# Value products of 64 rows with p copied by ScalarE alone, and the shifted feed-forward input sent behind the scores

## The chip, the cores and the metric

One NeuronCore of a Trainium2 chip. The time is device microseconds, the median of three runs. The kernel is one launch with no work on the host.

## The reference

The input x is 2 sequences of 1024 tokens of 128 features (2048 tokens, or 16 tiles of 128 tokens). A stack of six transformer layers runs twice on it, with one scan layer between the two passes:

- x = x + 0.5 * stack(layernorm(x))
- x = x + scan_layer(layernorm(x)): a 128x128 projection, a first-order recurrence over the tokens, and another 128x128 projection
- x = x + 0.5 * stack(layernorm(x))

Each stack layer does, in float32:

- shift: the upper 64 features of a token are replaced by those of the token before it
- local attention with 16 heads of 64: q, k, v = shifted x @ Wqkv (128 x 3072). q and k are scaled to unit length and rotated. Windows of 32 tokens attend to themselves and to the window before (32 queries against 64 keys), with a causal mask, softmax, and the product with v; then @ Wo (1024 x 128) and the residual
- feed-forward: shift again, layernorm, @ W1 (128 x 682), a * gelu(gate), @ W2 (341 x 128), residual.

## The kernel before

A step handles one tile of 128 tokens at each stage of a software pipeline. There are 12 passes of a layer over 16 tiles, so T = 192 tiles and about 198 steps, fully unrolled. In step s an engine works on several tiles at once: tile s-1 is projected to q and k (L_QKV), s-2 gets its values and scores (L_S), s-3 its softmax (L_SM), s-4 the product p v and the output projection (L_AV, L_WO), s-5 the first half of the feed-forward (L_F), s-6 the second (L_F2), and tile s is transposed in (L_X). "k.on(L)" starts the part of a stage, and "k.wait(sem, L)" waits until the semaphore's event has happened for the tile at that stage. Each engine executes its part of the step in the written order of its function step(k); between engines only these semaphores order anything. No planner is involved. Around step 102, over some twenty steps, the scan layer is threaded in (middle(k)): more work for VectorE and GpSimd.

One step on each engine, in order:

- TensorE: q/k projection chunks 1 and 0 (line 484), transposes of q (495), the products p v (attend, 539), chunks 2 and 3 (484), transposes of k (495), output projection (594), transposes of p (602), transpose of the normalised feed-forward input xn (607), second feed-forward product (622), values chunks 1 and 0 (490), transpose of the next tile (639), first feed-forward products (503), mask (519) and scores (527).
- ScalarE: squares (673), exp (686), copies of qT, oT, kT out of PSUM (691, 695, 711), xn (715), its half of the copy of p (722), xnT (727), the values (677), gelu with its table load (740), and the shifted next tile xsT (747 to 750).
- VectorE: swp and rot for chunks 0 and 1 (861, 867) with bn_aggr (932) and the epsilon (937) between them, the row sums of p (940), nb (945), the reciprocal (949), two reductions of the squares (954, 957) with chunk 3 between them, chunk 2, a chain of small reciprocal-root operations (816 to 848) with the two residual additions (969, 979) among them, its half of the copy of p (992), middle(k), the gate product hT (1001), the row maximum (1008) and the subtraction (1011), and bn_stats of the shifted input xs2 (1016).
- GpSimd: a power for the layernorm (1074), the normalisation of p (1078), rot+swp (1084), and rot times the inverse norm (1093).
- SyncE's DMA queue: vb (the values of the window before, 447 and 448), weights (357, 361), and the shift, four transfers from Z to xs2 (405 to 408), issued once the first residual addition (969, semaphore v_z1) is done.

The operand pT of the products p v has 128 rows, of which half are zeros: the four windows of a tile are handled in pairs, a pair shares one product with K = 128, and the block that belongs to the other window is zero. pT is cleared once and only the non-zero quarters are written, rows 0 to 63 by ScalarE (722) and rows 64 to 127, with neighbouring 32-blocks exchanged, by VectorE (992). A product has 64 columns of weights (the values) and 64 moving columns, 32 products a step. A float32 product shows as two LDWEIGHTS and two MATMUL records in the trace, a transpose as one of each.

Semaphores that the steps of the prediction name: v_ab[c] says that rot chunk c is written; values(k, 0) needs v_ab[2] and values(k, 1) needs v_ab[3], since they write over the same PSUM bank. a_v is the copied values, a_xT the transposed next tile, p_S the scores, p_O the products p v, v_nb the bias for xn, d_xs2 the arrival of the shift.

Of the kernel before, what the change touches and what calls it, by code (L numbers as in the profile page):

```python
# [57 lines left out]
def macaron(nc, x_in, w_in, w_out, b_out, w_qkv, q_scale, k_scale, w_o,  # L58
            w_1, w_2, b_2, c_cols, c_rope, c_mask, c_ident, out):
    with ExitStack() as ctx:  # L60
# [16 lines left out]
        pT = sb("pT", [PAIRS * 2, 2, 2, WIN])  # L77
# [64 lines left out]
        c_pz = sem("c_pz")  # L142
        v_pT = sem("v_pT")
# [210 lines left out]
        def _(sp):  # L354
# [81 lines left out]
            def step(k):  # L436
                if k.reg is not None:

                    for lag in (L_X, L_WO):
                        k.slot(lag), k.slot(lag, 0, P // 2), k.slot(lag, 1, P // 2)  # L440
                if k.on(L_SM):


                    k.wait(a_v[0], L_SM)
                    k.wait(p_O, L_AV)
                    par = k.parity(L_SM)
                    sp.dma_start(vb[WIN:P, :], va[0:P - WIN, par, :]).then_inc(d_vb, 16)
                    sp.dma_start(vb[0:WIN, :], va[P - WIN:P, 1 - par, :]).then_inc(d_vb, 16)
                load_weights(k)
                if k.on(L_WO):  # L450


                    k.wait(v_z1, L_WO)
                    shift(k, L_WO, xs2[:, :], d_xs2)
                if k.reg is None and k.s >= OUT:
                    t = k.s - OUT
                    sp.wait_ge(f_out, t + 1)
                    sp.dma_start(out[t // POS, (t % POS) * P:(t % POS + 1) * P, :], xb[:, t, :]).then_inc(d_out, 16)
# [9 lines left out]
        def _(pe):  # L468
# [62 lines left out]
            def attend(k):  # L531
                par = k.parity(L_AV)
                for p in range(PAIRS):
                    o4 = ops[:, p // 4, (p % 4) * P:(p % 4 + 1) * P].rearrange("p (t g i) -> p t g i", t=2, g=2)
                    for g in range(2):
                        for hp in range(2):
                            at = (2 * p + hp) * DH
                            v = vb[:, at:at + DH] if g == 0 else va[:, par, at:at + DH]
                            last = mm(o4[hp * DH:(hp + 1) * DH, :, g, :], v,  # L539
                                      pT[:, 2 * p + g, hp, :, :].rearrange("p t i -> p (t i)"),  # L540
                                      start=True, stop=True, skip_group_check=True)
                last.then_inc(p_O, 1)

            def step(k):
# [87 lines left out]
                if k.on(L_X):  # L632
                    k.wait(v_z1, L_WO)
                    if k.mid(M_T) is not None:
                        k.wait_mid(m_xn, M_T)
                        tr(ops[:, 0, 2 * P:3 * P], mx_n[:, :], idf[:, :])
# [31 lines left out]
        def _(act):  # L668
# [10 lines left out]
            def step(k):  # L679
# [12 lines left out]
                if k.on(L_AV):  # L692
                    k.wait(p_O, L_AV)
                    k.wait(p_wo, L_WO + 1)
                    cp(oT[:, :, :], ops[:, :, :].rearrange("p b (a x) -> p (b a) x", x=P)).then_inc(a_oT, 1)  # L695
# [20 lines left out]
                if k.on(L_SM):  # L716

                    k.wait(p_pT, L_SM)
                    k.wait(p_O, L_AV)
                    if k.s == L_SM:  # L720
                        act.wait_ge(c_pz, 1)
                    cp(pT[0:DH, :, :, 0, :], tps[0:DH, :, :].rearrange("p c (g h i) -> p (c g) h i", g=2, i=WIN)).then_inc(a_pT, 1)  # L722
# [20 lines left out]
                if k.on(L_X):  # L743
# [3 lines left out]
                    cp(xsT[0:hf, par, 0:P], ops[0:hf, 0, P:2 * P])  # L747
                    cp(xsT[hf:P, par, 1:P + 1], ops[hf:P, 0, P:2 * P])
# [3 lines left out]
                if k.mid(M_T) is not None:  # L752

                    k.wait(p_xT, L_X)
                    cp(mx_t[:, :], ops[:, 0, 2 * P:3 * P]).then_inc(m_xT, 1)
# [27 lines left out]
        def _(dve):  # L783
# [135 lines left out]
            def step(k):  # L919
# [22 lines left out]
                if k.on(L_F):  # L942
                    k.wait(g_rstd, L_F)
                    k.wait(a_xn, L_F + 1)
                    v.tensor_scalar(nb[:, 0:1], mv[:, 0:1], rt2[:, 1:2], -1.0, ALU.mult, ALU.mult).then_inc(v_nb, 1)
                if k.on(L_SM):
                    k.wait(v_sum, L_SM)
                    k.wait(g_nrm, L_SM + 1)
                    v.reciprocal(rr[:, :], rs[:, :]).then_inc(v_rec, 1)  # L949
                if k.on(L_QKV):  # L950
# [7 lines left out]
                    rotate(k, 3, False)  # L958
                    rsqrt(k, 1)
# [23 lines left out]
                if k.on(L_SM):  # L983

                    if k.s == L_SM:
                        dve.wait_ge(c_pz, 1)
                    k.wait(p_pT, L_SM)
                    k.wait(p_O, L_AV)
                    src = tps[DH:P, :, :]
                    swapped = bass.AP(src.tensor, src.offset + WIN,  # L990
                                      [list(src.ap[0]), [2 * WIN, 2 * PAIRS], [-WIN, 2], [1, WIN]])
                    v.tensor_copy(pT[DH:P, :, :, 1, :], swapped).then_inc(v_pT, 1)
# [60 lines left out]
        def _(pool):  # L1053
# [16 lines left out]
            def step(k):  # L1070
                if k.on(L_F):
                    k.wait(v_ve, L_F)
                    k.wait(a_xn, L_F + 1)
                    g_.tensor_tensor(rt2[:, 1:2], rt2[:, 0:1], half[:, 0:1], ALU.pow).then_inc(g_rstd, 1)  # L1074
                if k.on(L_SM):
# [3 lines left out]
                                     ALU.mult).then_inc(g_nrm, 1)  # L1079
                if k.on(L_QKV):  # L1080
# [73 lines left out]
            def between(s):  # L1154

                if s == 0:
                    g_.memset(pT[:, :, :, :, :], 0.0).then_inc(c_pz, 1)
# [72 lines left out]
```

## Time and profile before

| | us |
|---|---|
| median of 3 runs | 3302.99 (3298.94 to 3304.68) |
| the profiled execution | 3302.78 |
| its span, first to last instruction | 3301.0 |

TensorE was granted 0.994 of its full clock on average. The page gives PE 3177.7 us of busy time, DVE 2994.8, ACT 2543.2 and POOL 2229.6. PE is TensorE's matmuls, PEld its weight loads, DVE is VectorE, ACT ScalarE, POOL GpSimd, SP SyncE. A busy PE is a modelled figure, since matmuls overlap. In a timeline row the first number is the start and the second the length in us, then come engine, line, operation, output and input, and in brackets the idle time before it with what ended it. On VectorE and ScalarE a record lasts some 0.1 us beyond the start of the next one when they run back to back, so the distance of two starts, and not the length, is what an operation costs there.

### The profile page before, as it was taken

The numbers are of one execution on the slowest core, as the hardware profiler recorded it, in microseconds if no ns is written. First come the engines' busy times: TensorE is split into PE (matmuls) and PEld (weight loads), VectorE is DVE, ScalarE is ACT, GpSimd is POOL, SyncE is SP. The second block draws the span as 40 slices with busy tenths as digits, with TensorE's granted clock in tenths as the row PEclk, the third lists the DMA queues.
The fourth block names the chain that finished last, engine by engine and source line by source line (L and its number), as shares of the span: only waits on it lengthen the run. The fifth ranks groups of instructions, "written<-read, shape, count | busy, mean of one in ns | idle before, by whom it ended". The sixth has DMA issues, their size and how long they took to land. (4 is left out here: it accounts for less than half of the span.)

```text
span 3301.0 us, 125954 instructions
## 1 busy us (share of the span) xinstructions
PE 3177.7 (96%) x50984; PEld 2377.1 (72%) x51176; DVE 2994.8 (91%) x7143; ACT 2543.2 (77%) x4144; POOL 2229.6 (68%) x1454
## 2 busy tenths in 40 slices
PE   7999999999999999999889999999999999999998
PEld 3777777777777777776667777777777777777776
DVE  7999999999899999999999998899999999999995
ACT  3877878777787777777667777788777777887775
POOL 6666666666666666667777766666666666666663
PEclk9999999999999999999999999999999999999999
DMA  4111111111111111111111111111111111111111
GB/s 124 44 48 44 48 45 48 45 48 44 47 45 48 45 48 45 47 44 39 37 37 47 45 48 45 40 48 46 45 44 48 45 48 45 48 45 48 47 52 38
DMA packets 134996, 155.84 MB, mean 47 GB/s; under 512 B 75539, under 2 KB 108439, under 8 KB 134423
## 3 DMA queue, kind: packets, MB, share of 16 engines
q1 hardware_dynamic: 129815, 144.42, 15.9%
q8 instruction: 413, 6.77, 0.9%
q10 hardware_dynamic: 4608, 3.34, 0.4%
q14 instruction: 160, 1.31, 0.1%
HBM read 33.38 MB, written 1.05 MB: 10 GB/s over the span
## 5 line engine op out<-in xcount | busy, mean ns | idle before, releaser
L1084 POOL TENSOR_TENSOR rot<-rot,swp 128x1024 f32<-128x1024 f32 x384 | 907.2, 2363 | 132.5 <-DVE rot L867 132.5
L484 PE MATMUL proj<-wq,xsT 128*128 128x512 f32 x1536 | 773.4, 622 | 55.9 <-DVE hT L1001 22.4
L673 ACT ACTIVATE sq<-proj 128x512 f32<-128x512 f32 x768 | 437.6, 596 | 400.6 <-PE proj L484 387.3
L1093 POOL TENSOR_TENSOR rot<-rot,rn 128x1024 f32<-128x1024 f32 x384 | 724.6, 1910 | 0.0
L1074 POOL TENSOR_TENSOR rt<-rt,half 128x1 f32<-128x1 f32 x192 | 105.8, 551 | 743.1 <-DVE rt L937 743.1
L861 DVE TENSOR_TENSOR swp<-proj,tab 128x512 f32<-128x512 f32 x768 | 522.0, 680 | 9.4 <-ACT sq L673 5.1
L867 DVE TENSOR_TENSOR rot<-proj,tab 128x512 f32<-128x512 f32 x768 | 518.9, 676 | 1.7 <-PE tps L495 1.6
L495 PEld LDWEIGHTS tps<-idf,rot 128*128 128x128 f32 x3072 | 362.6, 141 | 207.1 <-issue 205.1
L1078 POOL TENSOR_TENSOR prob<-prob,rr 128x1024 f32<-128x1024 f32 x192 | 365.8, 1905 | 174.7 <-DVE rr L949 174.7
L484 PEld LDWEIGHTS proj<-wq,xsT 128*128 128x128 f32 x1536 | 257.5, 189 | 293.0 <-issue 138.1
L495 PE MATMUL tps<-idf,rot 128*128 128x128 f32 x3072 | 402.0, 274 | 3.5 <-POOL rot L1093 1.9
L594 PE MATMUL ops<-wo,oT 128*128 128x128 f32 x3072 | 376.3, 276 | 4.0 <-ACT oT L695 4.0
L539 PE MATMUL ops<-pT,vb 128*64 128x64 f32 x6144 | 379.3, 225 | 0.0
L490 PE MATMUL proj<-wq,xsT 128*128 128x512 f32 x768 | 369.5, 601 | 3.5 <-DVE rot L867 3.3
L539 PE MATMUL ops<-pT,va 128*64 128x64 f32 x6144 | 369.6, 222 | 0.0
L594 PEld LDWEIGHTS ops<-wo,oT 128*128 128x128 f32 x3072 | 359.8, 193 | 4.3 <-issue 4.2
L527 PEld LDWEIGHTS sps<-kT,qT 64*32 64x32 f32 x24576 | 258.4, 105 | 121.5 <-issue 121.1
L722 ACT COPY pT<-tps 64x1024 f32<-64x1024 f32 x192 | 193.2, 1006 | 187.3 <-PE tps L602 187.3
L1001 DVE SCALAR_TENSOR_TENSOR hT<-proj,cols,fg 114x128 f32<-114x128 f32 (+1 forms) x576 | 166.8, 345 | 187.4 <-issue 179.1
L539 PEld LDWEIGHTS ops<-pT,vb 128*64 128x64 f32 x6144 | 311.6, 138 | 32.9 <-issue 32.6
L527 PE MATMUL sps<-kT,qT 64*32 64x64 f32 x24576 | 296.2, 225 | 33.3 <-issue 33.2
L503 PEld LDWEIGHTS proj<-xnT,w 128*114 128x114 f32 (+1 forms) x2304 | 273.5, 178 | 73.7 <-issue 67.9
(104 smaller groups left out, 6164.6 us busy)
## 6 DMA issues: line engine op xcount, KB each, us to landing
vb<-va SPq DMA_DIRECT2D x192, 384.0 KB, 3.5
vb<-va SPq DMA_DIRECT2D x192, 128.0 KB, 3.6
wq<-in_L_ffn_Wqkv SPq DMA_DIRECT2D x95, 192.0 KB, 3.4
xs<-Z SPq DMA_DIRECT2D x192, 32.0 KB
wo<-in_L_ffn_Wo SPq DMA_DIRECT2D x94, 64.0 KB, 2.8
xs<-Z SPq DMA_DIRECT2D x192, 28.0 KB
xs<-Z SPq DMA_DIRECT2D x192, 3.8 KB
xs<-Z SPq DMA_DIRECT2D x192, 0.2 KB
```

Source lines behind the costliest of these rows:

```text
L484: mm(proj[:, c % 2, :], xsT[:, k.parity(L_QKV), 0:P], wq2[:, bass.ds(w + c * 512, 512)], start=True, stop=True).then_inc(p_qkv[c], 1)
L490: mm(proj[:, c, :], xsT[:, k.parity(L_S), 0:P], wq2[:, bass.ds(w + (4 + c) * 512, 512)], start=True, stop=True).then_inc(p_v[c], 1)
L495: last = tr(tps[:, p, :], rot[:, g * INNER + p * P:g * INNER + (p + 1) * P], idf[:, :])
L527: last = mm(sps[to:to + WIN, ty, p * 64:(p + 1) * 64], qT[rows, p, w * WIN:(w + 1) * WIN], kT[rows, p, at:at + 2 * WIN], start=False, stop ...
L539: last = mm(o4[hp * DH:(hp + 1) * DH, :, g, :], v, pT[:, 2 * p + g, hp, :, :].rearrange("p t i -> p (t i)"), start=True, stop=True, skip_g ...
L594: last = mm(ops[:, 0, 0:P], oT[:, p, :], wo[:, bass.ds(w + p * P, P)], start=(p == 0), stop=(p == PAIRS - 1))
L673: fn(sq[:, c * 512:(c + 1) * 512], proj[:, c % 2, :], ACT.Square).then_inc(a_sq[c], 1)
L861: v.tensor_tensor(halves(swp[:, c * 512:(c + 1) * 512]), swapped, tab[:, bass.ds(po + (2 * g + 1) * POS * DH, DH)] .rearrange("p (a d) -> ...
L867: v.tensor_tensor(heads(rot[:, c * 512:(c + 1) * 512]), heads(src), tab[:, bass.ds(po + 2 * g * POS * DH, DH)].unsqueeze(1) .to_broadcast( ...
L1078: g_.tensor_tensor(pr, pr, rr[:, :].unsqueeze(2).to_broadcast([P, HEADS, 2 * WIN]), ALU.mult).then_inc(g_nrm, 1)
L1084: g_.tensor_tensor(r, r, swp[:, g * INNER:(g + 1) * INNER], ALU.add).then_inc(g_add[g], 1)
L1093: g_.tensor_tensor(r, r, rn[:, g * HEADS:(g + 1) * HEADS].unsqueeze(2) .to_broadcast([P, HEADS, DH]), ALU.mult).then_inc(g_nm[g], 1)
```

## The change

1. pT becomes 128 x 8 x 128 without padding. Each product p v of K = 128 with 64 moving columns is split in two of K = 64 with 32 moving columns, one for each row half t, which write to two different PSUM banks. There are 64 products a step in place of 32.
2. The copy of p out of PSUM is one ScalarE copy of 128 x 1024; VectorE's copy (992), its semaphore v_pT, and the clearing of pT with c_pz are gone. oT is read with another order of its elements.
3. The shift's four transfers wait for p_S of the same step as well.
4. bn_stats (1016) moves from the end of VectorE's step to the next step behind the rotations of chunks 0 and 1. bn_aggr follows the row sums, the epsilon the reciprocal, and nb comes behind the last rotation of chunk 3. On GpSimd the power (1074) comes behind the normalisation of p (1078).
5. On TensorE the transpose of xn comes behind the second feed-forward product, and the transposes of the next tile go to the bank of tps in place of ops, behind waits for a_kT and a_pT in place of v_z1.

```diff
@@ sync, step
                     k.wait(v_z1, L_WO)
+                    k.wait(p_S, L_S)
                     shift(k, L_WO, xs2[:, :], d_xs2)
@@ tensor, attend
-                    o4 = ops[:, p // 4, (p % 4) * P:(p % 4 + 1) * P].rearrange("p (t g i) -> p t g i", t=2, g=2)
...
-                            v = vb[:, at:at + DH] if g == 0 else va[:, par, at:at + DH]
-                            last = mm(o4[hp * DH:(hp + 1) * DH, :, g, :], v,
-                                      pT[:, 2 * p + g, hp, :, :].rearrange("p t i -> p (t i)"),
-                                      start=True, stop=True, skip_group_check=True)
+                            for t in range(2):
+                                o4 = ops[:, t, p * 64:(p + 1) * 64].rearrange("p (g i) -> p g i", g=2)
+                                at = (2 * p + hp) * DH
+                                rows = slice(t * DH, (t + 1) * DH)
+                                v = vb[rows, at:at + DH] if g == 0 else va[rows, par, at:at + DH]
+                                to = (2 * g + (hp ^ t)) * WIN
+                                last = mm(o4[hp * DH:(hp + 1) * DH, g, :], v, pT[rows, p, to:to + WIN],
+                                          start=True, stop=True, skip_group_check=True)
@@ tensor, step
-                    k.wait(v_pT, L_AV)
...
-                if k.on(L_F):
-                    k.wait(a_xn, L_F)
-                    k.wait(v_sub, L_S + 1)
-                    tr(sps[:, 1, 0:P], xn[:, :], idf[:, :]).then_inc(p_xnT, 1)
                 if k.on(L_F2):
...
                     last.then_inc(p_f2, 1)
+                if k.on(L_F):
+                    k.wait(a_xn, L_F)
+                    k.wait(v_sub, L_S + 1)
+                    tr(sps[:, 1, 0:P], xn[:, :], idf[:, :]).then_inc(p_xnT, 1)
...
                 if k.on(L_X):
-                    k.wait(v_z1, L_WO)
+                    k.wait(a_kT, L_S)
+                    k.wait(a_pT, L_SM)
...
-                    tr(ops[:, 0, P:2 * P], Z[:, bass.ds(k.slot(L_X), P)], idf[:, :]).then_inc(p_xT, 1)
+                    tr(tps[:, 4, :], Z[:, bass.ds(k.slot(L_X), P)], idf[:, :]).then_inc(p_xT, 1)
@@ scalar, step
-                    cp(pT[0:DH, :, :, 0, :], tps[0:DH, :, :].rearrange("p c (g h i) -> p (c g) h i", g=2, i=WIN)).then_inc(a_pT, 1)
+                    cp(pT[:, :, :], tps[:, :, :]).then_inc(a_pT, 1)
@@ vector, step
                     rotate(k, 0, True)
                     rotate(k, 0, False)
-                if k.on(L_F):
-                    k.wait(v_bn, L_F)
-                if k.on(L_QKV):
                     rotate(k, 1, True)
-                if k.on(L_F):
-                    v.bn_aggr(mv[:, :], st[:, :]).then_inc(v_mv, 1)
-                if k.on(L_QKV):
                     rotate(k, 1, False)
                 if k.on(L_F):
-                    k.wait(v_mv, L_F)
-                    v.tensor_scalar(rt2[:, 0:1], mv[:, 1:2], 1e-5, None, ALU.add).then_inc(v_ve, 1)
+                    k.wait(d_xs2, L_F, per=64)
+                    v.bn_stats(st[:, :], xs2[:, :]).then_inc(v_bn, 1)
                 if k.on(L_SM):
                     k.wait(a_exp, L_SM)
                     v.tensor_reduce(rs[:, :], prob[:, :, :, :].rearrange("p a t j -> p (a t) j"), AX,
                                     ALU.add).then_inc(v_sum, 1)
                 if k.on(L_F):
-                    k.wait(g_rstd, L_F)
-                    k.wait(a_xn, L_F + 1)
-                    v.tensor_scalar(nb[:, 0:1], mv[:, 0:1], rt2[:, 1:2], -1.0, ALU.mult, ALU.mult).then_inc(v_nb, 1)
+                    k.wait(v_bn, L_F)
+                    v.bn_aggr(mv[:, :], st[:, :]).then_inc(v_mv, 1)
...
                     v.reciprocal(rr[:, :], rs[:, :]).then_inc(v_rec, 1)
+                if k.on(L_F):
+                    k.wait(v_mv, L_F)
+                    v.tensor_scalar(rt2[:, 0:1], mv[:, 1:2], 1e-5, None, ALU.add).then_inc(v_ve, 1)
...
                     rotate(k, 3, False)
+                if k.on(L_F):
+                    k.wait(g_rstd, L_F)
+                    k.wait(a_xn, L_F + 1)
+                    v.tensor_scalar(nb[:, 0:1], mv[:, 0:1], rt2[:, 1:2], -1.0, ALU.mult, ALU.mult).then_inc(v_nb, 1)
...
-                    v.tensor_copy(pT[DH:P, :, :, 1, :], swapped).then_inc(v_pT, 1)
...
-                if k.on(L_WO):
-                    k.wait(d_xs2, L_WO, per=64)
-                    v.bn_stats(st[:, :], xs2[:, :]).then_inc(v_bn, 1)
```

## Rows read from the trace of the kernel before

**Rows 1.** The page, busy time of each engine.

```profile
PE 3177.7 (96%) x50984; PEld 2377.1 (72%) x51176; DVE 2994.8 (91%) x7143; ACT 2543.2 (77%) x4144; POOL 2229.6 (68%) x1454
```

**Rows 2.** Timeline of VectorE, a step from 1163.57, the next from 1180.01.

```profile
1163.57 0.67 DVE L861 TENSOR_TENSOR swp<-proj,tab 128x512 f32<-128x512 f32 x1
...
1180.01 0.67 DVE L861 TENSOR_TENSOR swp<-proj,tab 128x512 f32<-128x512 f32 x1
...
1182.52 1.21 DVE L940 TENSOR_REDUCE rs<-prob 128x16 f32<-128x1024 f32 x1
1183.64 0.20 DVE L945 TENSOR_SCALAR nb<-mv,rt 128x1 f32<-128x1 f32 x1
...
1186.73 0.68 DVE L867 TENSOR_TENSOR rot<-proj,tab 128x512 f32<-128x512 f32 x1
...
1188.22 0.68 DVE L867 TENSOR_TENSOR rot<-proj,tab 128x512 f32<-128x512 f32 x1
...
1193.00 0.87 DVE L1001 SCALAR_TENSOR_TENSOR hT<-proj,cols,fg 114x128 f32<-114x128 f32 x3 [1.05 <-issue]
...
1196.17 0.28 DVE L1016 BATCH_NORM_STATS2 st<-xs 128x6 f32<-128x128 f32 x1
1196.37 0.68 DVE L861 TENSOR_TENSOR swp<-proj,tab 128x512 f32<-128x512 f32 x1
```

**Rows 3.** Timeline of TensorE, the same two steps.

```profile
1171.83 1.88 PE L490 MATMUL proj<-wq,xsT 128*128 128x512 f32 x4
...
1182.03 1.99 PE L484 MATMUL proj<-wq,xsT 128*128 128x512 f32 x4
...
1188.16 1.92 PE L490 MATMUL proj<-wq,xsT 128*128 128x512 f32 x4
...
1192.03 1.48 PE L527 MATMUL sps<-kT,qT 64*32 64x64 f32 x128
```

**Rows 4.** Timeline of ScalarE, the step from 1180.01.

```profile
1185.97 0.52 ACT L715 ACTIVATE xn<-xs,nb,rt 128x128 f32<-128x128 f32 x1
...
1190.11 0.59 ACT L677 COPY va<-proj 128x512 f32<-128x512 f32 x1 [0.23 <-PE proj L490]
...
1192.01 0.89 ACT L740 ACTIVATE fg<-proj,cols 114x128 f32<-114x128 f32 x3
...
1195.61 0.60 ACT L673 ACTIVATE sq<-proj 128x512 f32<-128x512 f32 x1 [0.20 <-PE proj L484]
```

**Rows 5.** Groups by line and shape: count, busy us, mean ns of one.

```profile
L539 PE MATMUL ops<-pT,vb 128*64 128x64 f32 x6144 | 379.3, 225 | 0.0
...
L527 PE MATMUL sps<-kT,qT 64*32 64x64 f32 x24576 | 296.2, 225 | 33.3 <-issue 33.2
```

**Rows 6.** Timeline of SyncE's queue, the step from 1180.01.

```profile
1189.22 0.52 SPq L405 DMA_DIRECT2D xs<-Z  x1
...
1191.30 0.55 SPq L408 DMA_DIRECT2D xs<-Z  x1
```

**Rows 7.** DMA issues: count, KB each, median us from issue to landing.

```profile
vb<-va SPq DMA_DIRECT2D x192, 128.0 KB, 3.6
...
out<-xb SPq DMA_DIRECT2D x16, 64.0 KB, 1.8
```

**Rows 8.** Windows: us, busy of PE, PEld, DVE, ACT, POOL; clock, DMA share.

```profile
1463.32:1516.63 53.31, 51.34 (x816) 37.25 (x819) 52.30 (x122) 40.74 (x67) 37.50 (x27) 1.00 0.17 45
1516.63:1753.39 236.76, 211.70 (x3245) 156.85 (x3255) 231.44 (x549) 162.37 (x271) 171.30 (x141) 0.97 0.14 39
1753.39:1823.41 70.02, 69.12 (x1087) 50.98 (x1089) 68.98 (x173) 53.74 (x90) 54.14 (x42) 1.00 0.16 43
```

**Rows 9.** Timeline of VectorE around its copy of p, a step of the middle.

```profile
1645.66 1.23 DVE L992 COPY pT<-tps 64x1024 f32<-64x1024 f32 x1
1646.92 0.29 DVE L880 TENSOR_TENSOR xb<-xb,ops 128x128 f32<-128x128 f32 x1
```

**Rows 10.** Waits of TensorE: us in total, times, longest.

```profile
PE sps L527 <- issue: 33.2, 35, 1.5
```

More of the change, by code:

```diff
@@ L76, in macaron @@
         prob = sb("prob", [PAIRS, 2, 2 * WIN])
-        pT = sb("pT", [PAIRS * 2, 2, 2, WIN])
+        pT = sb("pT", [PAIRS, P])
         oT = sb("oT", [PAIRS, P])
@@ L141, in macaron @@
         c_zero, c_zero2 = sem("c_zero"), sem("c_zero2")
-        c_pz = sem("c_pz")
-        v_pT = sem("v_pT")
         s_idb, s_mask = sem("s_idb"), sem("s_mask")
@@ L533, in attend @@
                 for p in range(PAIRS):
-                    o4 = ops[:, p // 4, (p % 4) * P:(p % 4 + 1) * P].rearrange("p (t g i) -> p t g i", t=2, g=2)
                     for g in range(2):
                         for hp in range(2):
-                            at = (2 * p + hp) * DH
-                            v = vb[:, at:at + DH] if g == 0 else va[:, par, at:at + DH]
-                            last = mm(o4[hp * DH:(hp + 1) * DH, :, g, :], v,
-                                      pT[:, 2 * p + g, hp, :, :].rearrange("p t i -> p (t i)"),
-                                      start=True, stop=True, skip_group_check=True)
+                            for t in range(2):
[6 more added lines that the diff above has]
+                                          start=True, stop=True, skip_group_check=True)
                 last.then_inc(p_O, 1)
@@ L632, in step @@
                 if k.on(L_X):
-                    k.wait(v_z1, L_WO)
+                    k.wait(a_kT, L_S)
+                    k.wait(a_pT, L_SM)
                     if k.mid(M_T) is not None:
                         k.wait_mid(m_xn, M_T)
-                        tr(ops[:, 0, 2 * P:3 * P], mx_n[:, :], idf[:, :])
+                        tr(tps[:, 5, :], mx_n[:, :], idf[:, :])
                     k.wait(v_z, L_X)
                     k.wait_mid(m_z, TILES)
-                    tr(ops[:, 0, P:2 * P], Z[:, bass.ds(k.slot(L_X), P)], idf[:, :]).then_inc(p_xT, 1)
+                    tr(tps[:, 4, :], Z[:, bass.ds(k.slot(L_X), P)], idf[:, :]).then_inc(p_xT, 1)
                 if k.on(L_F):
@@ L694, in step @@
                     k.wait(p_wo, L_WO + 1)
-                    cp(oT[:, :, :], ops[:, :, :].rearrange("p b (a x) -> p (b a) x", x=P)).then_inc(a_oT, 1)
+                    cp(oT[:, :, :].rearrange("p a (t x) -> p t a x", t=2),
+                       ops[:, :, :].rearrange("p t (a x) -> p t a x", x=2 * WIN)).then_inc(a_oT, 1)
                 if k.on(L_QKV):
@@ L719, in step @@
                     k.wait(p_O, L_AV)
-                    if k.s == L_SM:
-                        act.wait_ge(c_pz, 1)
-                    cp(pT[0:DH, :, :, 0, :], tps[0:DH, :, :].rearrange("p c (g h i) -> p (c g) h i", g=2, i=WIN)).then_inc(a_pT, 1)
+                    cp(pT[:, :, :], tps[:, :, :]).then_inc(a_pT, 1)
                 if k.on(L_F):
@@ L746, in step @@
                     hf, par = P // 2, k.parity(L_X)
-                    cp(xsT[0:hf, par, 0:P], ops[0:hf, 0, P:2 * P])
-                    cp(xsT[hf:P, par, 1:P + 1], ops[hf:P, 0, P:2 * P])
+                    cp(xsT[0:hf, par, 0:P], tps[0:hf, 4, :])
+                    cp(xsT[hf:P, par, 1:P + 1], tps[hf:P, 4, :])
                     k.wait(a_xT, L_X + 1)
@@ L754, in step @@
                     k.wait(p_xT, L_X)
-                    cp(mx_t[:, :], ops[:, 0, 2 * P:3 * P]).then_inc(m_xT, 1)
+                    cp(mx_t[:, :], tps[:, 5, :]).then_inc(m_xT, 1)
             def between(s):
@@ L958, in step @@
                     rotate(k, 3, False)
+                if k.on(L_F):
+                    k.wait(g_rstd, L_F)
+                    k.wait(a_xn, L_F + 1)
+                    v.tensor_scalar(nb[:, 0:1], mv[:, 0:1], rt2[:, 1:2], -1.0, ALU.mult, ALU.mult).then_inc(v_nb, 1)
+                if k.on(L_QKV):
                     rsqrt(k, 1)
@@ L982, in step @@
                         rsqrt(k, n)
[L983 to L991, printed above, removed]
-                    v.tensor_copy(pT[DH:P, :, :, 1, :], swapped).then_inc(v_pT, 1)
                 middle(k)
@@ L1070, in step @@
             def step(k):
[L1071 to L1074, printed above, removed]
                 if k.on(L_SM):
@@ L1079, in step @@
                                      ALU.mult).then_inc(g_nrm, 1)
+                if k.on(L_F):
+                    k.wait(v_ve, L_F)
+                    k.wait(a_xn, L_F + 1)
+                    g_.tensor_tensor(rt2[:, 1:2], rt2[:, 0:1], half[:, 0:1], ALU.pow).then_inc(g_rstd, 1)
                 if k.on(L_QKV):
@@ L1154, in between @@
             def between(s):
-                if s == 0:
-                    g_.memset(pT[:, :, :, :, :], 0.0).then_inc(c_pz, 1)
                 if s in (1, 2):
```

## The prediction

> **What bounds the kernel now.** The page's busy times come first: TensorE 96%, VectorE 91% [rows 1]. That would suggest a kernel bound by TensorE, so the timelines of two ordinary steps are read next. A step is measured from one start of swp chunk 0 on VectorE to the next: 1163.57 to 1180.01 is 16.44 us, and 1180.01 to 1196.37 is 16.36 [rows 2]; odd and even steps differ in one small ScalarE operation. With R = 1180.01, the chain that closes the loop is this. VectorE runs without a gap from R to the end of rot chunk 2, at 1188.22 + 0.68 = 1188.90, R+8.89 [rows 2]. That releases the last values product, and the values end on TensorE at 1188.16 + 1.92 = 1190.08, R+10.07, 1.18 after the release [rows 3]. ScalarE's copy starts at 1190.11, then come the table load and gelu, ending 1192.90, and after them the three small copies for xsT. q/k chunks 1 and 0 of the next step wait for xsT, and the square of chunk 0 ends at 1195.61 + 0.60 = 1196.21 [rows 4]. VectorE starts the next step at 1196.37. Between, it idles 1.05 us before hT, which waits for gelu (1192.90, start 1193.00) [rows 2, 4]. From hT to the subtraction and bn_stats it runs without a gap, so at the step's end two legs meet: bn_stats starts at 1196.17 and costs 0.20, and the square is ready at 1196.21 [rows 2, 4]. The loop is therefore VectorE, TensorE, ScalarE, TensorE, ScalarE, and neither the products p v nor VectorE's copy of p is in it: the copy lies just ahead of the 1.05 us of idle time. TensorE looks 96% busy because its work is spread to meet each release just in time.
>
> **The change part by part.** *VectorE's copy of p goes.* In an ordinary step it buys nothing: VectorE idles 1.05 + 1.2 us before hT instead, because hT waits for gelu and gelu for the values. ScalarE's copy takes the same time for 128 rows as for 64, since the same 1024 columns pass.
>
> *bn_stats moves.* It leaves the short leg behind hT and enters the long one, ahead of rot chunk 2. There it adds 0.20 [rows 2]. Once nb no longer lies behind the row sums, the reciprocal waits some 0.03 for them (row sums start 1182.52, last 1.21, nb came at 1183.64). nb itself stays ahead of rot chunk 2. So rot chunk 2 ends at R+9.12. At the other end the next step now waits for the square alone: 1196.21 plus a handover of 0.10, as between gelu and hT, is 1196.31 and not 1196.37, 0.06 earlier. Even step: +0.23 - 0.06 = +0.17. Odd step: its values ended at 1171.83 + 1.88 = 1173.71, R+10.14, where TensorE and not VectorE held them [rows 2, 3]; now 9.12 + 1.18 = 10.30, +0.16, less 0.07 at the end, is +0.09. The mean is +0.13 a step.
>
> *nb moves, and the transpose of xn with it.* xn waits for nb, the transpose for xn, and the values stand behind the transpose in TensorE's queue. nb starts 0.60 behind the last rot of chunk 3 (1186.73, R+6.72, now R+6.83), so at R+7.43, and ends R+7.63. xn takes 0.52 [rows 4], to R+8.19; transpose R+8.24; values from R+8.35, their third record (the one that needs rot chunk 2) at R+9.21. Rot chunk 2 allows it at 9.12 + 0.1. The two tie, so this costs nothing more; each 0.1 us that nb or xn is later costs 0.1 a step. On GpSimd the power now stands behind the normalisation of p, some 2 us, and ends near R+6.6, still ahead of nb.
>
> *The products p v.* Now 64 records of 64 moving columns, two column halves side by side, from R to the next projection at 1182.03 (R+2.02) less some 0.15 of turnaround: 1.87 us, 58 ns a pair [rows 3, 5]. After, 128 records of 32 columns on four quarters of the array. The lower end is the pace of the scores, 128 records in 1.48 us on eight parts [rows 3, 5]; the upper end is that the row halves don't overlap, 64 pairs of 58 ns, 3.7 us. I take 1.9: the weights still have 64 columns as in the row of line 539, and four quarters then take what two halves took for twice the size. Anything up to about 2.3 us is free: q/k chunk 3 would be late, but the second reduction of squares has about 0.5 us of slack. The Trainium skill's page "TensorEngine Tiling (Array Packing)", section Instruction Overhead, speaks against the change: a matmul costs some 60 cycles however few columns it has, so halving the columns would save nothing per record, and 128 records at 25 ns would be an estimated 3.2 us if they didn't overlap. The trace has 128 records in 1.48 us, 11.6 ns each, so by this case's row that floor isn't one for the whole array.
>
> *The shift waits for the scores.* Its first issue moves from 1189.22 (R+9.21) to the end of the scores, 1192.03 + 1.48 = 1193.51, with +0.23 of the longer step R+13.75 [rows 3, 6]. The last of the four issues starts 2.08 later and lands between 1.8 us (the output's median) and 3.6 us (vb's) after that [rows 6, 7], so 3.9 to 5.7 us behind the first. bn_stats needs it at R+2.36 of the next step, with a step of 16.53 that is 5.1 us behind the first issue. Mostly it is there; where an instruction fetch or another transfer is in its way it isn't. I take a wait of 0.27 in three steps of ten, 0.08 a step. The ends are 0 and 0.6 (always 5.7). Behind bn_stats stands all of VectorE, on the long leg, so each wait is paid in full. SyncE's next vb transfers need p_O, R+2.1, by when the four are issued.
>
> *The steps with the scan layer.* Here VectorE bounds: twelve steps take 236.76 us (19.7 each) with 231.44 of it busy, and three before and four behind take 53.31 and 70.02 (17.8 and 17.5) [rows 8]. The copy of p costs 1646.92 - 1645.66 = 1.26 there [rows 9]. Twelve times 1.26 is 15; three times 1.25 is 3.7; the last four fall only to the ordinary 16.53, 3.9. Together -23. bn_stats costs the same at either place here.
>
> *TensorE's instructions.* 128 more a step to fetch. The scores wait for "issue" 35 times, 33 us in all [rows 10]: their 256 instructions pass in 1.48 us, quicker than they come. The shift's transfers no longer run then, which should shorten it; the products p v are a second such burst, with slack behind it. I take -5; bounds -20 and +15. The transposes of the next tile wait for the copy of p (about R+9.2) and come at R+10.1: nothing. First and last steps: -1.
>
> Sum: own time 3302.8; 165 ordinary steps at +0.13, +21; 184 at +0.08, +15; -23; -5; -1: 3309.8, so 3310, 7 us (0.2%) above the median 3303, which the profiled execution's 3302.8 matches.
>
> **The rivals.** *Slow products p v.* The halves don't overlap: 3.7 us, 1.85 more. oT's copy and chunk 3 would wait; after 0.45 of slack some 1.4 a step reach the loop, 190 x 1.4 = 266: 3570. For it: these shapes are nowhere in the trace. Against: the scores overlap row halves.
>
> *The shift always late.* If each step waits for xs2 0.3 to 0.6 us, 190 x 0.3 is 57 in place of 15: 3350 (up to 3410). It decides from 5.1 us behind the first issue. For: vb's median of 3.6. Against: the four are small.
>
> *The loop doesn't lengthen, or the fetches gain.* If the waits for xs2 are nil (-15) and the scores' stalls shrink to a third (-15), the middle's 23 us stand against the 21: 3285. This is the other side. The case needs both.
>
> *TensorE bounds after all.* By the 96% [rows 1], a burst at the scores' pace saves 0.4 of 1.87 in 190 steps, -75, with the middle 3215. Behind it stands a rule of the Trainium skill, page "TensorE: Matmul & The Clock Gate", section Part 3: Packing small matmuls: weight loads overlap running matmuls only where the row group differs, so alternating row halves should free the array. By that rule the old products would have paid each load beside its matmul, which the 58 ns a pair in the trace don't show. Against it: the handovers above leave TensorE no place in the loop at line 539.
>
> **How the numbers follow.** Chances: forecast 0.50 (own range 3297 to 3323), late shift 0.12, slow products 0.05, gains 0.27, TensorE 0.06. Measurements tell 0.2%, 6.6 us, from no change: faster is below 3296.4, slower above 3309.6. The forecast case gives 0.26 slower, 0.22 same, 0.02 faster; the gains 0.21 faster, 0.06 same; TensorE 0.06 faster; the other two 0.17 slower. Faster 0.29, same 0.28, slower 0.43. The range 3282 to 3345 leaves out the two outer rivals and the worst of the late shifts.
>
> **What would show it.** Right: ordinary steps of 16.5 to 16.6 us; VectorE idle for some 2.2 us before hT; xn starting near R+7.7; the middle's long steps near 18.5; TensorE's busy share down without a gain; bn_stats waiting for the DMA in a part of the steps; the products p v in 1.5 to 2.3 us. Wrong: a step below 16.36, the products in 3 us or more, or bn_stats waiting in most steps.

## The result, and the profile after

The changed kernel takes 3358.18 us (median of 4 runs, 3352.09 to 3366.07) against 3303.84 in the same session, a ratio of 1.0169 (95% interval 1.0145 to 1.0193). It is 54 us slower. The forecast was 3310 with a range of 3282 to 3345: the sign was right, the time lies outside the range.

The page of the changed kernel, engines' busy time and the queue that brings the instructions; the last line is that queue in the kernel before (packets, MB, share):

```profile
PE 3216.1 (96%) x63464; PEld 2383.5 (71%) x63464; DVE 2780.6 (83%) x6951; ACT 2541.6 (76%) x4144; POOL 2219.7 (66%) x1453
...
q8 instruction: 509, 8.34, 1.1%
```

```profile
q8 instruction: 413, 6.77, 0.9%
```

VectorE is 214 us less busy than in [rows 1], and yet the kernel is slower. The instruction queue moved 96 packets more for 128 x 192 = 24,576 more TensorE instructions: one packet of 16 KB for each 256 instructions. (The counts of the two pages differ by 192 more, since one MATMUL record a step is missing from the old trace; with it the old kernel has 105,723 instructions on TensorE, and 413 packets hold 105,728.) That line matters below.

**An undisturbed step is what was forecast.** First VectorE, one step of the changed kernel (it answers to [rows 2]; start, length, then engine and line):

```profile
542.18 0.69 DVE L861 TENSOR_TENSOR swp<-proj,tab 128x512 f32<-128x512 f32 x1
...
544.59 0.28 DVE L931 BATCH_NORM_STATS2 st<-xs 128x6 f32<-128x128 f32 x1
...
549.68 0.20 DVE L958 TENSOR_SCALAR nb<-mv,rt 128x1 f32<-128x1 f32 x1
...
550.69 0.68 DVE L867 TENSOR_TENSOR rot<-proj,tab 128x512 f32<-128x512 f32 x1
...
555.46 0.87 DVE L992 SCALAR_TENSOR_TENSOR hT<-proj,cols,fg 114x128 f32<-114x128 f32 x3 [2.31 <-ACT fg L740]
...
558.76 0.69 DVE L861 TENSOR_TENSOR swp<-proj,tab 128x512 f32<-128x512 f32 x1
```

TensorE in the same step (as [rows 3]):

```profile
542.27 0.32 PE L541 MATMUL ops<-pT,vb 64*64 64x32 f32 x8
...
544.04 0.30 PE L541 MATMUL ops<-pT,va 64*64 64x32 f32 x8
544.26 1.98 PE L483 MATMUL proj<-wq,xsT 128*128 128x512 f32 x4
...
550.62 1.92 PE L489 MATMUL proj<-wq,xsT 128*128 128x512 f32 x4
...
554.49 1.49 PE L526 MATMUL sps<-kT,qT 64*32 64x64 f32 x128
```

And ScalarE (as [rows 4]):

```profile
549.91 0.49 ACT L717 ACTIVATE xn<-xs,nb,rt 128x128 f32<-128x128 f32 x1 [1.19 <-DVE nb L958]
...
551.77 0.58 ACT L678 COPY va<-proj 128x512 f32<-128x512 f32 x1
```

With R = 542.18 the step is 16.58 us (forecast 16.53). rot chunk 2 ends at 551.37, R+9.19 (9.12), xn starts at R+7.73 (7.7), the values end at 552.54, R+10.36 (10.30), VectorE idles 2.31 before hT (2.2), and the products p v pass in 544.26 - 542.27 = 1.99 us with the turnaround (1.9 + 0.15). bn_stats, at R+2.41, is in the long leg.

**What surrounds it is not.** The waits of the changed kernel (us in total, times, longest):

```profile
DVE hT L992 <- ACT fg L740: 403.3, 179, 4.4
...
DVE mx L999 <- PE sps L526: 64.1, 67, 4.2
PE sps L526 <- issue: 63.4, 68, 1.8
...
DVE st L931 <- DMA xs<-Z: 25.5, 27, 3.5
...
PE ops L541 <- issue: 6.8, 14, 1.6
```

The scores' waits for issue went from 33.2 us in 35 places [rows 10] to 63.4 in 68, and VectorE waits behind them for the same 64 us. One such step, TensorE and then VectorE:

```profile
759.27 0.68 PE L526 MATMUL sps<-kT,qT 64*32 64x64 f32 x46
761.24 0.43 PE L526 MATMUL sps<-kT,qT 64*32 64x64 f32 x25 [1.29 <-issue]
```

```profile
761.75 1.22 DVE L999 TENSOR_REDUCE mx<-sps 128x16 f32<-128x1024 f32 x1 [1.20 <-PE sps L526]
```

The burst stops within the scores for 1.29 us with nothing to wait for but its own instructions, and the row maximum is late by 1.20. The transfers of that stretch, 759.0 to 760.1, show the instruction queue at work (packets, MB, share of the 16 engines):

```profile
q8 instruction: 1, 0.02, 5.4%
```

Its one packet runs from 759.08 to 760.04, and TensorE goes on 1.20 us behind its end.

And a step in which the shift is late, SyncE's queue and VectorE:

```profile
828.02 0.53 SPq L403 DMA_DIRECT2D xs<-Z  x1
...
830.22 0.55 SPq L406 DMA_DIRECT2D xs<-Z  x1
```

```profile
832.53 0.68 DVE L867 TENSOR_TENSOR rot<-proj,tab 128x512 f32<-128x512 f32 x1
833.99 0.30 DVE L931 BATCH_NORM_STATS2 st<-xs 128x6 f32<-128x128 f32 x1 [0.78 <-DMA xs<-Z]
```

The transfer is there some 5.9 us behind the first issue (833.9 less 828.02), against the 5.1 that the forecast gave it.

To weigh them I took every step from one swp of chunk 0 to the next, numbered from 0, and set apart the 160 ordinary ones (steps 6 to 83 and 106 to 187) from the 22 around the scan layer (84 to 105). Time lost inside the scores is how much longer than 1.48 us they take:

| | before | after | difference |
|---|---|---|---|
| an undisturbed ordinary step | 16.37 / 16.44 | 16.58 | +0.18 x 160 = +29 |
| time lost inside the scores, ordinary steps | 36.5 us in 34 | 66.4 us in 59 | +30 |
| bn_stats late for xs2, ordinary steps | 0 | 20.1 us in 23 | +20 |
| mean of the 22 steps around the scan layer | 18.65 | 17.58 | -23 |

The sum is +56; the medians are 54 apart. The 160 ordinary steps themselves take 2737.9 us instead of 2660.1, so +78 where the three parts give +79.

The windows of the scan layer in the changed kernel, cut at the same steps as [rows 8]:

```profile
1496.00:1548.53 52.53, 50.07 (x993) 37.16 (x991) 46.45 (x118) 40.12 (x67) 36.44 (x26) 1.00 0.17 47
1548.53:1761.93 213.40, 205.89 (x4041) 154.21 (x4042) 209.05 (x536) 162.41 (x271) 170.67 (x141) 1.00 0.16 44
1761.93:1832.25 70.32, 67.21 (x1331) 51.27 (x1324) 62.78 (x168) 53.37 (x90) 54.89 (x45) 1.00 0.16 44
```

The column of the clock, the third from the end, matters here: 1.00 in the twelve long steps, where [rows 8] have 0.97. In the kernel before, the granted clock fell to half (1.2 GHz) for 3.4 us four times in these steps, once here:

```profile
1691.30:1694.70 3.40, 3.40 (x18) 2.18 (x18) 2.97 (x5) 2.00 (x3) 1.22 (x3) 0.50 0.00 0
```

Ahead of that fall TensorE had been busy for 15.05 of 17.40 us (1673.90 to 1691.30). The step behind each of the four falls takes 20.3 us, the others 19.4 to 19.5. So some 4 x 0.8 = 3.2 us of the fall from 236.76 to 213.40 came with the clock, which the changed kernel kept at 1.00 there.

### The profile page after: what moved, and what is told of

Same layout as the page of the kernel before. It is cut to its first block and busy times, and to the rows that moved or that the text cites. A ratio compares the mean times of both kernels' runs of the same rounds, so it can differ in the third digit from the quotient of the medians.

```text
span 3357.5 us, 150531 instructions
## 1 busy us (share of the span) xinstructions
PE 3216.1 (96%) x63464; PEld 2383.5 (71%) x63464; DVE 2780.6 (83%) x6951; ACT 2541.6 (76%) x4144; POOL 2219.7 (66%) x1453
## 5 line engine op out<-in xcount | busy, mean ns | idle before, releaser
L541 PE MATMUL ops<-pT,vb 64*64 64x32 f32 x12288 | 380.1, 220 | 4.6 <-issue 4.4
L541 PE MATMUL ops<-pT,va 64*64 64x32 f32 x12288 | 377.8, 219 | 2.9 <-issue 2.4
L526 PE MATMUL sps<-kT,qT 64*32 64x64 f32 x24576 | 302.0, 226 | 63.7 <-issue 63.4
L541 PEld LDWEIGHTS ops<-pT,vb 64*64 64x64 f32 x12288 | 330.4, 135 | 37.9 <-issue 37.6
L541 PEld LDWEIGHTS ops<-pT,va 64*64 64x64 f32 x12288 | 332.7, 135 | 4.1 <-issue 3.7
L502 PE MATMUL proj<-xnT,w 128*114 128x128 f32 (+1 forms) x2304 | 311.9, 285 | 1.8 <-ACT xnT L727 1.8
```

What stands on the lines that cost most here:

```text
L502: last = mm(proj[0:rows, a, c * P:(c + 1) * P], w1[:, at + a * FH + c * FC:at + a * FH + c * FC + rows], xnT[:, :], start=True, stop=True, ...
L526: last = mm(sps[to:to + WIN, ty, p * 64:(p + 1) * 64], qT[rows, p, w * WIN:(w + 1) * WIN], kT[rows, p, at:at + 2 * WIN], start=False, stop ...
L541: last = mm(o4[hp * DH:(hp + 1) * DH, g, :], v, pT[rows, p, to:to + WIN], start=True, stop=True, skip_group_check=True)
```

## The experiments

Each was timed beside the kernel before, whose median was 3303.78 for the first four, 3305.72 for the next three and 3305.3 for the last two.

**e1: products and copy alone, in the old order.** Parts 1 and 2 of the change, nothing else.

```diff
+                            for t in range(2):
...
+                                last = mm(o4[hp * DH:(hp + 1) * DH, g, :], v, pT[rows, p, to:to + WIN], ...)
...
+                    cp(pT[:, :, :], tps[:, :, :]).then_inc(a_pT, 1)
```

> The kernel before with only the 64-row products and the single ScalarE copy; shift, bn_stats, nb and the transpose of xn stay in their old places. 676 less about 0 instructions a step on TensorE in place of 549. Theory A (the instruction count makes the extra waits inside the scores): ordinary steps 16.37 and 16.44 as before when undisturbed, waits inside the scores 60 to 70 us in all instead of 36, the middle 23 us shorter, no wait for xs2: 3305 to 3315. Theory B (the new order makes them, by its waits and by the shift's transfers behind the scores): score waits stay near 36 us, 3280.

Measured: 3309.35, ratio 1.0015 (1.0005 to 1.0024). Its wait for the scores:

```profile
PE sps L525 <- issue: 61.6, 69, 1.8
```

An undisturbed step is as before (16.37 / 16.42), none waits for xs2, and the ordinary steps are 0.21 longer on average, +34 in 160, nearly all of it waits for issue (64.8 us in the scores, 9.7 in the products p v, the latter partly covered). The steps around the scan layer give back 22 x 1.31 = 29.

**e2: the order alone, with the padded products.** Parts 3 and 4, and the transpose of xn.

```diff
+                    k.wait(p_S, L_S)
                     shift(k, L_WO, xs2[:, :], d_xs2)
...
-                if k.on(L_WO):
-                    k.wait(d_xs2, L_WO, per=64)
-                    v.bn_stats(st[:, :], xs2[:, :]).then_inc(v_bn, 1)
```

> The kernel before with only the new order: shift behind p_S, bn_stats and nb moved, GpSimd's power behind the normalisation, transpose of xn behind the second product; padded products and VectorE's copy stay. TensorE's instruction count stays near 549 a step. Theory A (count): score waits stay near 36 us, undisturbed step 16.58, waits for xs2 some 20 us, middle as before: 3303 + 29 + 20 = 3350. Theory B (order): score waits rise to 66 us as well: 3380.

Measured: 3352.0, ratio 1.0138 (1.0121 to 1.0155).

```profile
PE sps L528 <- issue: 34.5, 35, 1.7
...
DVE st L932 <- DMA xs<-Z: 15.2, 27, 1.7
```

The undisturbed step is 16.58. The scores' waits are those of [rows 10], although the shift's transfers no longer run beside them: those transfers had no part in the waits. That the time came so near the expected 3350 is in part luck. The waits for xs2 are 15.2 us and not 20, and the 22 steps around the scan layer, expected as before, take 8 us more (19.03 us each): eight of the twelve long ones take 20.4 to 20.5 us, at a granted clock of 0.94 in 1537.70 to 1759.60.

**e3: the whole change, the shift issued early.**

```diff
-                    k.wait(p_S, L_S)
                     shift(k, L_WO, xs2[:, :], d_xs2)
```

> The changed kernel without the shift's wait for p_S: the four transfers go out right behind the first residual addition again. Both theories of the loop: the undisturbed step stays 16.58, since bn_stats and nb stay in their new places, and the waits for xs2 (20 us) vanish: 3338. If the shift's transfers beside the instruction fetches matter, the waits inside the scores change with it (66 us in the changed kernel): longer ones give up to 3355, and if the late transfers caused them, 3308.

Measured: 3337.77, ratio 1.0095 (1.008 to 1.011). The wait of bn_stats is gone (0.1 us in all), the undisturbed step is still 16.58. So the three runs split the loss: products and copy +5.6 (e1), the rest of the order +28.4 (e3 less e1), the wait for p_S +20.4 (the changed kernel less e3).

**e4: the kernel before with 128 TensorE instructions more a step**, 32 products of one column ahead of the products p v, written over at once.

```diff
+                for n in range(32):
...
+                    mm(ops[at:at + 1, 0, 0:1], idf[:, 0:1], idf[:, 0:1], start=True, stop=True, ...)
```

> The kernel before with 32 more float32 products of one row and one column a step ahead of the products p v (128 instructions more: 677 a step), whose results are overwritten. Theory A (count): waits inside the scores rise from 36 to 60 or 70 us, plus what the small products cost on the loop, under 0.4 us a step if they fit the slack ahead of q/k chunk 3: 3330 to 3400 and the score waits read from the trace decide. Theory B: score waits stay near 36 us.

Measured: 3433.57, ratio 1.0389 (1.0373 to 1.0404).

```profile
PE sps L527 <- issue: 67.8, 69, 1.8
```

The scores' waits double with the padded products too, so the shape of the split products isn't what makes them. The 128 instructions more are common to e1 and e4, and so is their place, at the products p v: a run that adds them elsewhere isn't there. The rest of the time was a miss. The small products delay the products p v by 0.57 us, and nearly all of it reaches the step (16.9 to 17.1); with the waits that is the 130 us. The slack that the forecast saw there (up to 0.4 us of longer products free) isn't there in the old order.

**g1: split products and the single copy in the 21 tiles 84 to 104 alone**, where VectorE bounds.

```diff
+SPLIT = range(84, 105)
...
-                    attend(k)
+                    (attend_split if k.tile(L_AV) in SPLIT else attend)(k)
...
-                if k.on(L_SM):
+                if k.on(L_SM) and k.tile(L_SM) not in SPLIT:
```

> The kernel before, except that tiles 84 to 104 (the ones whose copy of p falls in the steps with the scan layer) use the unpadded products and the single ScalarE copy, in a buffer of their own. Theory A (instruction count makes the score waits, VectorE's copy bounds only in the middle): ordinary steps 16.37 and 16.44 with about 36 us of score waits as before, the middle's 22 steps 1.0 to 1.3 us shorter each as in the changed kernel, 23 to 28 us less: 3276 to 3282. Rival (the split's gain in the middle is taken back by its extra fetches there): 3290 to 3300.

Measured: 3270.1, ratio 0.9886 (0.9867 to 0.9904; five runs, 3266.96 to 3275.93). That beats both kernels, and by more than expected. The twelve long steps:

```profile
1515.24:1726.40 211.16, 205.21 (x4038) 154.21 (x4050) 207.56 (x536) 162.63 (x271) 170.62 (x141) 1.00 0.16 44
```

17.6 us each, where 236.76 / 12 = 19.7 [rows 8] less the copy's 1.26 [rows 9] would be 18.5. More went than the copy. Some 0.3 us a step is the clock, 1.00 here; h1 and h2 are about the rest.

**g2 and g3: where the 256th instruction falls.** After e1 and e4 I looked at where in the scores the gap lies. Counting TensorE's instructions of a step (549 before, 676 after), the gap of every stalled step of the changed kernel up to the scan layer falls on the same number modulo 256, counted from the start of the program. That is the packet of the instruction queue: the engine runs out at a boundary. The trace shows the packets too. In steps 6 to 83, in all 14 such stops of the kernel before and all 26 of the changed one, TensorE goes on 1.2 to 1.5 us behind the end of the queue's latest packet. At the boundaries in the last 96 instructions that it passes, that packet had ended 1.4 to 6.5 us ahead in the kernel before (14 of them) and 1.2 to 1.6 us in the changed one (4). So what stops the engine is a packet that comes late. It stops only where the boundary lies some 160 to 255 instructions into the 256 of the scores. g2 is e3 with 23 small products more a step, which makes 768 = 3 x 256, so that the boundaries stay at one place, instruction 18 of the scores; it also leaves out, behind the scan layer, the waits that repeat a value already waited for. g3 has 16 products more in one early step, which moves them to instruction 210.

```diff
-                    if t >= 0:
+                    if t >= 0 and self.s - lag - (N - TILES) <= TILES + 1:
...
+                for n in range(23):
...
+                    mm(ops[at:at + 1, 0, 0:1], idf[:, 0:1], idf[:, 0:1], start=True, stop=True, ...)
```
```diff
-                for n in range(23):
+                for n in range(23 + (16 if k.s == 5 else 0)):
```

> The changed kernel with the early shift, plus 23 float32 products of one row and one column a step ahead of the products p v (92 instructions: 768 a step, three blocks of 256), and semaphore waits that repeat a value already waited for left out behind the middle. The block boundaries then keep their place from step to step; read from the changed kernel's trace they should fall on instruction 18 of the scores. Theory (a wait comes exactly where a boundary falls between about instructions 160 and 255 of the scores): no score wait in any ordinary step up to the middle, 69 us less in all than early_shift's sum if it holds behind the middle too; the small products cost some 0.3 us a step: 3310 to 3330. Rival (a mere count of instructions a step, wherever the boundaries fall): 3400 or more, waits in a third or more of the steps.

> As 768_apart, with 16 more small products once, in step 5, which moves every later boundary back by 64 instructions, to about instruction 210 of the scores. Theory: a wait of 1.0 to 1.5 us in every ordinary step up to the middle, some 80 x 1.2 = 95 us above 768_apart if behind the middle nothing changes. Rival: the same time as 768_apart within 5 us.

Measured: g2 3488.54 (1.0546, 1.0497 to 1.0595), g3 3571.97 (1.0798, 1.0767 to 1.0829). Two waits of g2:

```profile
PE ops L544 <- issue: 111.7, 140, 1.8
...
PE sps L525 <- issue: 7.5, 7, 1.5
```

and TensorE in two neighbouring steps of g3:

```profile
864.26 1.28 PE L525 MATMUL sps<-kT,qT 64*32 64x64 f32 x105
866.50 0.42 PE L525 MATMUL sps<-kT,qT 64*32 64x64 f32 x23 [0.96 <-issue]
...
882.14 1.28 PE L525 MATMUL sps<-kT,qT 64*32 64x64 f32 x105
884.93 0.42 PE L525 MATMUL sps<-kT,qT 64*32 64x64 f32 x23 [1.51 <-issue]
```

In g3 the scores stop behind the 105th MATMUL record, instruction 210, in every ordinary step up to the scan layer; in g2 they don't stop in any ordinary step. That part came as expected. g2's time was a miss. Its next boundary falls into the products p v (behind the 76th of their 128 MATMUL records, or the 97th after the scan layer), which now follow 92 small instructions and are with them a second long burst. Of the 111.7 us of waits there, 99 fall into ordinary steps, and the small products cost some 0.4 us a step. I had worked out the place in one burst and left the other out. A part of g2's time goes with the clock: behind the scan layer the granted clock fell to 1.2 GHz for 3.4 us or more in 19 ordinary steps, and these take 20.0 us on average, the other 63 there 17.8. Its two runs, 3473.52 and 3503.56, had a mean clock of 0.989 and 0.984. g3 lies 83 us above g2, where some 95 were expected; with 30 us between g2's own runs that says no more than that the rival, the same time within 5 us, is out.

**h1 and h2: the scan ahead of GpSimd's last product.** In the long steps GpSimd's rot times rn and two VectorE operations run at once. These are GpSimd and VectorE in a long step of the kernel before, then in an early step of the scan layer:

```profile
1646.64 1.92 POOL L1093 TENSOR_TENSOR rot<-rot,rn 128x1024 f32<-128x1024 f32 x1
```

```profile
1647.45 1.25 DVE L889 SCALAR_TENSOR_TENSOR xb<-Z,xb 128x128 f32<-128x128 f32 x1
...
1649.02 1.72 DVE L902 TENSOR_TENSOR_SCAN ys<-siga,ys,mbh 128x128 f32<-128x128 f32 x1
```

```profile
1475.02 1.92 POOL L1093 TENSOR_TENSOR rot<-rot,rn 128x1024 f32<-128x1024 f32 x1
```

```profile
1475.31 1.77 DVE L889 SCALAR_TENSOR_TENSOR xb<-Z,xb 128x128 f32<-128x128 f32 x1
```

The same operation takes 1.25 or 1.77 us, and ends both times 0.14 behind GpSimd's (1648.70 against 1648.56, 1477.08 against 1476.94). The scan ends 0.28 behind GpSimd's second product (1650.74 against 1650.46), which this row of the two together gives:

```profile
1646.64 3.82 POOL L1093 TENSOR_TENSOR rot<-rot,rn 128x1024 f32<-128x1024 f32 x2
```

In g1 the copy no longer lies ahead of it, and it meets GpSimd at another point, GpSimd and VectorE again:

```profile
1667.75 1.90 POOL L1119 TENSOR_TENSOR rot<-rot,rn 128x1024 f32<-128x1024 f32 x1
```

```profile
1667.12 0.36 DVE L915 SCALAR_TENSOR_TENSOR xb<-Z,xb 128x128 f32<-128x128 f32 x1
...
1667.80 2.14 DVE L928 TENSOR_TENSOR_SCAN ys<-siga,mbh 128x128 f32<-128x128 f32 x1
```

Now the sum takes 0.36, and the scan, 1.72 before, 2.14; it starts 0.05 behind GpSimd's product and ends 0.29 behind it. Two runs add one wait on GpSimd, for the scan of the same step, h1 to g1 and h2 to the kernel before:

```diff
                     k.wait(v_rs, L_QKV, per=RS_STEPS)
+                    k.wait_mid(m_y, M_IN)
                     for g in range(2):
```

> The version with split products in the scan-layer steps only, and one wait more there: GpSimd's product rot times the inverse norm waits for VectorE's scan of the same step. Theory H (a VectorE operation with two inputs in SBUF that starts beside a GpSimd operation ends only with it): in that version the scan starts 0.08 behind the end of rot+swp and table, and ends 0.28 behind the end of rot times norm (2.14 us each). Without GpSimd beside it it should take 0.3 to 1.2 us, so the long steps fall from 17.6 to 16.6 to 17.2 us, twelve of them, and the kernel from 3270 to 3255 to 3266. Rival R (the scan simply takes some 2 us, its length has nothing to do with GpSimd): the scan stays at 1.7 to 2.1 us, and GpSimd, 2 us later, makes the steps as long or longer: 3270 to 3290.

> The kernel before with the same single wait in the scan-layer steps, nothing else changed: VectorE's copy of p stays. Theory H: its residual sum xb (two inputs in SBUF) took 1.17 us because it ended with GpSimd's rot times norm, and the scan 1.64 for the same reason; with the wait they take about 0.3 and 0.3 to 1.2, so the long steps fall from 19.47 to 17.3 to 18.2 us, and the kernel to 3275 to 3290, although the copy is still there. Rival R (the lengths have nothing to do with GpSimd, the copy's 1.37 us were all that part 2 could remove): no step gets shorter, 3304 to 3330.

Measured: h1 3269.31 (0.989, 0.9873 to 0.9906), h2 3272.43 (0.9899, 0.9885 to 0.9914). A long step of h2, GpSimd and VectorE, and the window of its twelve long steps:

```profile
1635.32 3.76 POOL L1094 TENSOR_TENSOR rot<-rot,rn 128x1024 f32<-128x1024 f32 x2 [1.96 <-issue]
```

```profile
1634.12 0.28 DVE L889 SCALAR_TENSOR_TENSOR xb<-Z,xb 128x128 f32<-128x128 f32 x1
...
1634.71 0.47 DVE L902 TENSOR_TENSOR_SCAN ys<-siga,ys,mbh 128x128 f32<-128x128 f32 x1
```

```profile
1516.58:1725.74 209.16, 202.54 (x3233) 152.71 (x3243) 204.22 (x549) 161.83 (x271) 166.34 (x136) 1.00 0.16 44
```

The xb sum fell from 1.25 to 0.28, the scan from 1.72 to 0.47. The twelve steps fell from 236.76 to 209.16, 27.6 us (some 3.2 of it the clock, 1.00 here), and the kernel by 33: more than expected, for one wait, and with VectorE's copy of p still in place. The rival that these lengths are the operations' own is out. The Trainium skill, "SBUF — State Buffer", section Who interferes with whom, says just this: a VectorE instruction with two SBUF inputs contends with a GpSimd instruction that reads SBUF, and the one that starts later is blocked for the whole of the other. The trace agrees: the sum ends 0.14 us and the scan 0.28 us behind GpSimd's operation. In h1 the scan fell from 2.14 to 0.46 and its twelve long steps from 211.2 to 205.1, 17.1 us each as expected. The expected 3255 to 3266 was missed all the same: its median can't be told from g1's 3270.1, whose runs spread over 9 us. Taking the copy away and moving GpSimd's product take away much the same time.

## Why the prediction was wrong

- **The bound and the chain of the loop: right.** VectorE lost 214 us of busy time and its idle time before hT grew; no ordinary step got shorter for it.
- **"The mean is +0.13 a step": +0.18.** Each position came within 0.07 us of the forecast. e2 and e3 have the same 16.58 with and without the split products, so all of it is the order. +29 for +21.
- **nb, xn and the transpose as a tie: right.** The values' end is 0.06 later than forecast.
- **Products p v at 1.9: right**, 1.99 us with the turnaround, 15.5 ns a record. The rival of 3.7 us is out. The floor of the Trainium skill's page "TensorEngine Tiling (Array Packing)", section Instruction Overhead, an estimated 3.2 us by its figure, didn't hold here. That longer products would have been free was wrong for the old order (e4).
- **"I take a wait of 0.27 in three steps of ten, 0.08 a step": right in kind.** It came in one step of seven, but 0.87 us each: +20 for +15, and e3 shows +20.4 as its whole price.
- **"I take -5" for TensorE's instructions: this is the step that failed**, +30 for -5, beyond the bound of +15. Two reasons were wrong. The waits were thought to come from transfers in the way; e2 has these out of the way and the same 34.5 us. And the 128 instructions were thought to matter only in their own burst, which had slack; e1 and e4 show that with them another burst, the scores, stops more often. The boundary itself lies in the last 96 instructions of the scores as often as before (in 28 of the 78 ordinary steps ahead of the scan layer before, in 29 after). But before it stopped the engine in 14 of the 28, and below instruction 208 only in 3 of 13; in the changed kernel it did in 25 of the 29, and with e4's padded products in 28 of 30.
- **The middle, "together -23": right in sum, wrong in its parts.** The twelve long steps fell by 23.4 us, not 15; the three before by 0.8, not 3.7; the four behind not at all, where waits for issue and for xs2 took what the copy left (g1, without the new order, gets 28 in all). The 23.4 is not the copy alone; that the sum came out is luck. Some 3.2 us of it are the clock's four falls in the kernel before. In g1 a long step of 17.60 instead of 19.47 is made of 1.37 less for the copy and its handover, 0.89 less for the xb sum that GpSimd no longer held up, and 0.42 more for the scan that it now holds up longer.

One sum among the rivals is off too: stalls of 33 us that shrink to a third are -22 and not -15, which puts that side at 3278 and not 3285, below the range.

The corrected terms, +29 +20 +30 -23, give 3303 + 56 = 3359 against 3358 measured. With the one failed term at its forecast it would have been 3324, inside the range.

What stays open: what starts the transfer of the next packet, and why with 128 instructions more in a step it comes late at nearly every boundary in the last 96 instructions of the scores, where with 549 it is in time at half of them. That the place of the boundary decides over a wait is shown by g2 and g3, that the late packet is what the engine waits for by the packets' own times, and that the 128 instructions raise the waits by e1 and e4; the link between their number and the packet's lateness isn't shown.

## What to carry to other kernels

Where a burst of short TensorE instructions waits for "issue", count the instructions of a step modulo 256 and find the boundaries before adding any: here a change that halved the products' size doubled their number and paid in another burst. Look for one operation with two different lengths in the trace; when its end sticks to the end of another engine's operation, try to move one of them: here that was worth 33 us, about as much as taking VectorE's copy away (36). And a change that frees an engine only in one stage belongs in that stage alone: g1 is 1.1% faster with the products and the copy that leave the kernel 0.15% slower when every step has them (e1). When two versions are compared stage by stage, read the granted clock beside the time.

## What the runs showed of the hardware

- TensorE's instructions come in packets of 256 (96 packets more for 24,576 more). Where a packet's end falls late in a burst at 11.6 ns a record, the engine can stand still: for 0.9 to 1.5 us in g3, in every ordinary step up to the scan layer. It goes on 1.2 to 1.5 us behind the end of the transfer of the queue's latest packet (14 stops of the kernel before, 26 of the changed one).
- A VectorE operation with two SBUF inputs that starts beside GpSimd's rot times rn ends with it, whatever its own length: the sum 0.14 us behind it, 0.28 become 1.25 or 1.77, and the scan 0.28 us behind it, 0.47 become 1.72 or 2.14.
- Four quarters of the array take 64 x 32 products at 15.5 ns a record, against 11.6 for the scores' 64 x 64 products on eight parts.
- In the kernel before, TensorE's granted clock fell to 1.2 GHz four times in the twelve long steps, for 3.4 us each, and the step behind each fall was 0.8 us longer; in e2 eight of the twelve were some 0.9 us longer at a granted clock of 0.94. The changed kernel, g1 and h2 had 1.00 throughout these steps.
